# Attention over the unmasked tokens: projections a head earlier, one token transpose per head, gathers two batches ahead, all token sums on GpSimd

## What is computed

```python
xt = jnp.transpose(x, (0, 2, 1))
q = xt @ Wq.T                                   # 8 heads of 64
scores = scale * jnp.einsum('bhqd,bhkd->bhqk', qh, qh)
logits = (scores * cmask + (1.0 - cmask) * NEG) * rmask
attn = jax.nn.softmax(logits, axis=-1)
ctx = jnp.einsum('bhqk,bhkd->bhqd', attn, qh)
out = ctx @ Wo.T
x = x + jnp.transpose(out, (0, 2, 1))
```

## Time and profile before

| | us |
|---|---|
| median of 3 runs (1754.6 to 1766.28) | 1764.37 |
| the profiled execution | 1761.67 |
| its span, first to last instruction | 1759.9 |
| prologue and front, up to the first batch's loop | about 98 |
| one batch, mean of fifteen | 102.7 |

### The profile page before, as it was taken

The page is one execution under the profiler, slowest core; times in us unless marked ns, Lnnn a source line. Parts: engine busy times, 40 slices in busy tenths (PEclk is TensorE's granted clock), DMA queues, the critical chain, the costliest instruction groups (busy, mean ns, idle before and its releaser), DMA issues. The chain is left out here.

```text
span 1759.9 us, 33141 instructions
## 1 busy us (share of the span) xinstructions
PE 1585.6 (90%) x10956; PEld 1243.4 (71%) x10956; DVE 1285.5 (73%) x2794; ACT 853.9 (49%) x2055; POOL 1244.2 (71%) x979
## 2 busy tenths in 40 slices
PE   6798998989899898989989898998989899898995
PEld 3667777777777676767767677777777677677763
DVE  5458686777768687786877768687786868778673
ACT  1145554544555445455544545555454555545451
POOL 5266785868678587767868677686877768687672
PEclk9689999999999999999999999999999999999997
DMA  3244443535434354443444434344443534444320
GB/s 121 63 102 97 97 121 78 137 85 122 109 78 125 85 129 102 105 125 68 126 94 123 102 90 122 92 120 99 111 113 90 133 81 121 99 112 114 72 77 27
DMA packets 93809, 179.08 MB, mean 102 GB/s; under 512 B 24705, under 2 KB 24833, under 8 KB 93633
## 3 DMA queue, kind: packets, MB, share of 16 engines
q1 hardware_dynamic: 64448, 109.71, 27.1%
q0 software_dynamic: 29184, 67.17, 13.7%
HBM read 36.77 MB, written 33.55 MB: 40 GB/s over the span
## 5 line engine op out<-in xcount | busy, mean ns | idle before, releaser
L752 ACT ACTIVATE small_Pt<-scores,small_kbias 108x270 f32<-108x270 f32 x1280 | 552.6, 484 | 650.8 <-PE scores L1098 589.1
L884 DVE TENSOR_REDUCE small_mxp<-max_scores 108x1 f32<-108x270 f32 x1280 | 548.4, 433 | 313.9 <-PE max_scores L1080 295.0
L598 POOL TENSOR_TENSOR small_Pacc<-small_Pacc,small_Pt 108x540 f32<-108x540 f32 x384 | 521.1, 1357 | 223.7 <-ACT small_Pt L752 210.2
L1080 PE MATMUL max_scores<-small_ops 128*108 128x270 f32 x1280 | 435.3, 343 | 85.8 <-DMA small_ops<-small_L 43.1
L1080 PEld LDWEIGHTS max_scores<-small_ops 128*108 128x108 f32 x1280 | 226.4, 177 | 206.2 <-issue 77.3
L1110 PE MATMUL ctx_psum<-small_Pt,small_V 108*64 108x270 f32 x2560 | 313.0, 391 | 0.0
L914 DVE RECIPROCAL small_rsum<-small_rsum 128x67 f32<-128x67 f32 (+1 forms) x512 | 240.5, 532 | 57.3 <-ACT small_rsum L696 57.3
L1095 PE MATMUL scores<-small_ops 128*108 128x270 f32 x1280 | 275.0, 295 | 4.6 <-ACT small_Pt L752 3.1
L1098 PE MATMUL scores<-small_ops 128*108 128x270 f32 x1280 | 267.8, 291 | 0.0
L598 POOL TENSOR_TENSOR small_Pacc<-small_Pt 108x540 f32<-108x540 f32 x128 | 171.8, 1342 | 133.4 <-ACT small_Pt L752 128.6
L1110 PEld LDWEIGHTS ctx_psum<-small_Pt,small_V 108*64 108x64 f32 x2560 | 184.0, 137 | 107.5 <-issue 0.6
(11 more groups left out here) (106 smaller groups left out, 2316.9 us busy)
## 6 DMA issues: line engine op xcount, KB each, us to landing
small_ops<-small_H SPq DMA_DIRECT2D x512, 135.0 KB
small_ops<-small_L SPq DMA_DIRECT2D x256, 135.0 KB
small_ops<-small_mrow SPq DMA_DIRECT2D x128, 2.1 KB
small_xg<-x_rows,small_idx POOLq DMA_INDIRECT x80
small_xtail<-x_rows,small_idx POOLq DMA_INDIRECT x80
out_rows<-small_xtail,small_idx POOLq DMA_INDIRECT x80, 3.1
out_rows<-small_xg,small_idx POOLq DMA_INDIRECT x80
wq_sb<-wq SPq DMA_DIRECT2D x1, 1024.0 KB, 5.6
```

What stands on the lines that cost most here:

```text
L598: nc.gpsimd.tensor_tensor(acc, other, t["Pt"][:R, p0], ALU.add).then_inc(pacc_step, 1)
L752: nc.scalar.activation(t["Pt"][:R, (NT * s + k) % f.NP, half, :], ST[(2 * (NT * h + k) + half) % 3][:R, 0:H], ACT.Exp, bias=t["kbias"][:R, ...
L884: nc.vector.tensor_reduce(t["mxp"][:R, h % 2, m // 2, m % 2:m % 2 + 1], MX[m % 2][:R, 0:H], AX.X, ALU.max).then_inc(mx_red, 1)
L1080: nc.tensor.matmul(MX[m % 2][:R, 0:H], ops[:, OPA, tile_cols(m // 2)], ops[:, OPB, half_cols(m % 2)], start=True, stop=True).then_inc(mx_r ...
```

## The change

Six edits.

1. `PAIR_STEPS`: pair 3's first half from (0,4) to (0,3)-(0,4); pair 4's halves from (4,4) and (5,0)-(5,1) to (4,3) and (4,4); pair 5's first from (5,4) to (5,3)-(5,4).
2. `V_STEPS`: each of the two V parts has a place of its own. `XT_STEPS`: the token transposes go from (4,0) to (4,2), all in one head, to one in each of heads 1, 2 and 3, always (h,2) part 1, and two in head 4. The mean goes from (7,1) to (6,2), part 1.
3. Main tiles are gathered two batches ahead, in heads 6 and 7 (the third token buffer was there already), tail tiles one batch ahead in heads 2 and 3; a semaphore for even and one for odd batches. The prologue gathers batch 1 too. `MASKED_AT` goes from (3,3), (3,4) to (0,0), (0,1).
4. All token sums after the first batch's are on GpSimd: tail tiles in heads 4 and 5, the main tiles of the batch after next in head 7.
5. The masks of all 16 batches are made by three operations in the prologue.
6. The output tile is finished in place and not by way of the sum buffer, and the transposes use one identity matrix for both types.

```diff
 PAIR_STEPS = [
-    ((0, 0), (0, 1), "proj", (2, 1)), ((0, 4), (0, 4), "proj", (3, 0)), ((1, 0), (1, 1), "proj", (3, 1)),
+    ((0, 0), (0, 1), "proj", (2, 1)), ((0, 3), (0, 4), "proj", (3, 0)), ((1, 0), (1, 1), "proj", (3, 1)),
...
-    ((4, 4), (4, 4), "proj", (4, 0)), ((5, 0), (5, 1), "proj", (4, 1)), ((5, 4), (5, 4), "proj", (5, 0)),
+    ((4, 3), (4, 3), "proj", (4, 0)), ((4, 4), (4, 4), "proj", (4, 1)), ((5, 3), (5, 4), "proj", (5, 0)),
...
-V_STEPS = {1: (0, 3), 2: (4, 3), 3: (5, 3), 4: (6, 3)}
-XT_STEPS = [(4, 0, 0), (4, 0, 1), (4, 1, 0), (4, 1, 1), (4, 2, 0)]
-XBAR_STEP = (7, 1, 1)
+V_STEPS = {1: ((0, 2, 1), (0, 3, 0)), 2: ((4, 0, 0), (4, 0, 1)), 3: ((5, 0, 0), (5, 1, 0)), 4: ((6, 3, 0), (6, 4, 0))}
+XT_STEPS = [(1, 2, 1), (2, 2, 1), (3, 2, 1), (4, 1, 0), (4, 2, 1)]
+XBAR_STEP = (6, 2, 1)
...
-MASKS_AT = (2, 4, 1)
-MASKED_AT = [(3, 3), (3, 4)]
+MASKED_AT = [(0, 0), (0, 1)]
...
-VECTOR_SUM_AT = {1: (5, 0, 1), 2: (5, 1, 0), 3: (5, 1, 1), 4: (5, 4, 1), 5: (6, 0, 1), 6: (6, 1, 0)}
-POOL_SUM_AT = {7: (6, 1), 8: (6, 3), 9: (6, 4)}
+ADD_W_AT = [(0, 0), (0, 1), (0, 3), (0, 4), (1, 0)]
+SCATTER_TAIL_AT = [(1, 1), (1, 3), (1, 4), (2, 0), (2, 1)]
+GATHER_TAIL_AT = [(2, 3), (2, 4), (3, 0), (3, 1), (3, 3)]
+SCATTER_AT = [(3, 4), (4, 0), (4, 1), (5, 0), (5, 1)]
+TAIL_SUM_AT = [(4, 3), (4, 4), (5, 2), (5, 3), (5, 4)]
+GATHER_AT = [(6, 0), (6, 1), (6, 3), (6, 4), (7, 0)]
+SUM_AT = [(7, 1), (7, 2), (7, 3), (7, 4)]
+FIRST_SUM_AT = [(2, 1), (2, 2), (3, 1), (3, 2)]
...
                 def finish_tile(b, par, k, bank):
...
-                    nc.vector.scalar_tensor_tensor(out=t["xsum"][:R], in0=MB[bank][:R, 0:D],
-                                                   scalar=t["valid"][:R, slot, k:k + 1], in1=xk, op0=ALU.mult,
+                    nc.vector.scalar_tensor_tensor(out=xk, in0=MB[bank][:R, 0:D],
+                                                   scalar=t["valid"][:R, b, k:k + 1], in1=xk, op0=ALU.mult,
...
+                nc.vector.tensor_tensor(t["valid"][:], j, n, ALU.is_lt).then_inc(masks_made, 1)
+                nc.vector.tensor_tensor(t["inv"][:], j, n, ALU.is_ge).then_inc(masks_made, 1)
+                dve.wait_ge(masks_made, 2)
+                nc.vector.tensor_scalar(t["kbias"][:], t["inv"][:], NEG, None, ALU.mult).then_inc(masks_made, 1)
```

More of the change, by code:

```diff
@@ L111, in misc_jobs @@
     if form.split:
[L112 removed]
+        for pair, places in V_STEPS.items():
             if pair < PAIRS or has_next:
[L114 to L115 removed]
+                for i, (h, k, part) in enumerate(places):
+                    whole(part, "V", (pair, i), (h, k))
         for first, last, name, arg in PAIR_STEPS:
@@ L166, in pool_jobs @@
             if has_next:
-                table[GATHER_TAIL_AT[i]].append(("gather", NT + i))
+                table[GATHER_TAIL_AT[i]].append(("gather", 1, NT + i))
+                table[TAIL_SUM_AT[i]].append(("sum_tokens", 1, NT + i))
         for i in range(NT):
@@ L170, in pool_jobs @@
                 table[SCATTER_AT[i]].append(("scatter", i))
[L171 to L176, removed]
+            if has_third:
+                table[GATHER_AT[i]].append(("gather", 2, i))
+        for i in range(1, NT):
+            if has_third:
+                table[SUM_AT[i - 1]].append(("sum_tokens", 2, i))
+            if not has_prev:
+                table[FIRST_SUM_AT[i - 1]].append(("sum_tokens", 1, i))
         return table
@@ L184, in pool_jobs @@
         for i in range(NT):
-            table[gathers[i]].append(("gather", i))
+            table[gathers[i]].append(("gather", 1, i))
         for i in range(1, NT):
-            table[4 + (i - 1) // 3, (i - 1) % 3].append(("sum_tokens", i))
+            table[4 + (i - 1) // 3, (i - 1) % 3].append(("sum_tokens", 1, i))
     return table
@@ L567, in job @@
                     elif name == "gather":
-                        gather(b + 1, arg)
+                        gather(b + ahead, arg)
                     elif name == "add_w":
@@ L617, in body @@
                 nc.gpsimd.memset(t["ops"][DK:DK + 1, :, OPY, :].bitcast(F32), 1.0).then_inc(ops_cleared, 1)
+                if f.split:
+                    for k in range(NT):
+                        gather(1, k)
                 def batch(b, par, table, has_prev, has_next):
-                    jobs = pool_jobs(f, has_prev, has_next)
+                    jobs = pool_jobs(f, has_prev, has_next, b + 2 < B)
                     for h in range(HEADS):
@@ L624, in batch @@
                                 add_tile(HEADS * b + h, h, k)
-                            for name, arg in jobs[h, k]:
-                                job(name, arg, b, par)
+                            for name, *ahead, arg in jobs[h, k]:
+                                job(name, ahead[0] if ahead else 0, arg, b, par)
                 def tail(jobs):
@@ L1199, in job @@
                         row = CT[:NT, H:H + R] if f.split else mb[:NT, 0:R]
-                        nc.tensor.transpose(row, t["mcol"][:R, arg % 2, :], ident[:R, :R]).then_inc(mT_ready, 1)
+                        nc.tensor.transpose(row, t["mcol"][:R, arg % 2, :], identR[:R, :R].bitcast(F32)).then_inc(mT_ready, 1)
                     elif name == "L":
```

81 lines of the change are left out of this document (28 added, 53 removed).

## The result

| | before | changed |
|---|---|---|
| median, us | 1762.69 (1754.6 to 1766.28, 4 runs) | 2050.36 (2049.24 to 2050.8, 4 runs) |
| ratio, 95% interval | | 1.1635 (1.161 to 1.1661) |
| span of the profiled execution, us | 1759.9 | 2048.2 |

A forecast was written before the change was run, and what follows sets the result against it. TensorE's waits were taken to decide: 17.0 + 1.7 - 6.0 = 12.7 us a batch, 191 in 15 batches, plus 3 for the last and 46 for the clock, 240 in all, giving 2004 us; range 1870 to 2075.

The forecast's parts named there:

- The path: At (h,2), ScalarE copies row sums after value products, transposes and their copies, delaying VectorE; long waits total 17.0 us a batch.
- that of the banks: Experiments' rival theory: transposes and output products alternating on two banks cause the wait, whatever the sums' order; no chance given.
- Rival C: In heads 1 to 3 TensorE waits only for the reduction behind the reciprocals, one step later: 1885 us; chance 0.12.
- Rival A: The long path doesn't bind, or TensorE's waits overlap, so only the removals count: 1657 us; chance 0.06.
- Rival B: GpSimd sets the pace, its head 7 sums delaying L (the row-sum matmul): 1717 us; chance 0.03.
- D: Rival: long waits are a quarter of those worked out and cancel against the removals: 1764 us; chance 0.03.
- The waits for the low part: TensorE waits for VectorE's token tile low half: 3.7 us in heads 1 to 3, 3.1 at head 4's projection.
- the row maxima: In heads 0 and 6, maxima wait for the reduction behind the reciprocals: 1.4 us each, 2.8 a batch.
- L's 1.7 us: Row-sum matmul L waits for its bank: 0.6 us each in heads 2 and 3, 0.5 in heads 0, 1 and 6.
- The clock: New long waits lower TensorE's granted clock: 0 to 92 us, the upper being four times as much low clock; 46 taken.
- The removals: Operand wait, mean's wait, transposes' bank queue and half VectorE's wait go: 6.0 us a batch, 7.0 with clock.
- the projection's place: Pair 4's second projection ends at (4,4) instead of (5,1), removing the row maxima's operand wait: 2.9 us a batch.

The follow-up runs named there:

- e1: Changed kernel with ScalarE serving the row sums ahead of the step's other copies at (h,2): 1703.06 us, 0.9672 of before.
- e2: Changed kernel with head 0's V part, the transposes and the mean at (h,2) moved from part 1 to part 0: 1665.16 us, 0.9454 of before.
- e5: Kernel of e2 with head 0's V part and the mean back in part 1, ScalarE serving row sums ahead of their copies: 1637.41 us.
- e7: Kernel of e2 with six of a batch's nine token sums back on VectorE, four in head 7, two in head 4: 1699.14 us.
- e3: Changed kernel with the score products of (h,3) repeated six times in heads 1 to 3, five in head 4, to fill TensorE's waits: 1949.2 us.
- e6: Kernel of e2 with pair 4's projection halves back at (4,4) and (5,0) to (5,1), as before the change: 1676.52 us.
- e9: Kernel of e6 with three token sums on VectorE in head 5, at (5,0), (5,1) and (5,1): 1706.03 us.
- e4: Changed kernel with ScalarE's 0.63 us refill of the token tile buffer behind the row sums in heads 1 to 3: 2045.58 us.
- e10: Kernel of e2 with three token sums on VectorE in head 5, at (5,0), (5,1) and (5,1): 1721.1 us.

## Why the prediction was right, point by point

**Direction and mechanism: right, and shown.** The path goes as worked out. Counted from the start of the transposes (651.91 in the working, 736.19 in the changed trace):

| | worked out | measured |
|---|---|---|
| cast starts | 0.55 | 0.62 |
| row sums end | 2.06 | 2.14 |
| next reduction starts | 3.9 | 3.97 |
| low half ends | 4.8 | 4.85 |
| output product's wait | 3.7 | 3.70 |

The prediction's theory and that of the banks are kept apart by e1 and e2, which cure the two ends of the same order and both bring the time under before's. Rival C, that the output product's bank would not be what TensorE waits for, falls by the row that names it. Rival A named the right price for the removals alone: 1657, where e2 has 1665 and e5 1637, but its condition doesn't hold. Rival B falls by the changed kernel's waits, where L waits 0.3 us for GpSimd in all, and by e7; D falls by the result.

**Idle time: right within a tenth.** I had 12.7 us more a batch; 19.8 - 8.2 = 11.6 were measured. The waits for the low part were to be 3 x 3.7 + 3.1 = 14.2 a batch, 213 in all. The row has 204.5: fourteen batches have them as worked out, but the first batch has no output products, and so only the projection's wait, which I overlooked. At the row maxima I took 1.4 us each; head 6 has 1.47, head 0 has 1.07. L's 1.7 us is (15.9 + 11.3 + 7.6)/15 = 2.3 against 0.25 before; 7.6 of it is head 4's, where L takes the bank of a token tile, which I left out.

**The clock: this is the term that was mis-sized.** I bounded it at 0 and 92 us and took 46. Of 289 us, 15 x 11.6 = 174 are idle time, where the sum had 194, which leaves 115 for the clock, above even the upper bound of 92; e3 takes 101 away. The step that failed is "four times as much" as the upper bound, made from one long wait a batch. Low clock rose from 127 to 389 us in all, and in the stretches from 4.1 a batch to (1 - 0.91) x 2 x 1722/14 = 22, more than five times. In the 3.4 us behind the wait the clock was under 1.00 for every one of the long waits, and in all fifteen batches also for the 1.47 us wait of head 6, which I had not counted among its causes. For the 1.07 us wait of head 0 it stayed at 1.00 in all fifteen. Here is head 6 of batch 2, and below it the stretch behind head 0's wait in batch 3:

```profile
436.31 0.38 PE L1065 MATMUL max_scores<-small_ops 128*108 128x270 f32 x1 [1.47 <-DVE small_mxp L866]
436.60:440.00 3.40, 3.25 (x16) 2.97 (x15) 2.48 (x7) 1.98 (x6) 2.23 (x3) 0.51 0.47 118
...
462.32:465.72 3.40, 3.20 (x24) 3.02 (x25) 3.07 (x9) 2.40 (x6) 2.73 (x3) 1.00 0.35 79
```

So the range held the result by its upper part: forecast 2004, measured 2050. The clock was 69 us over its term and the idle time 20 under its own, and it was luck that the two errors partly cancel. By the Trainium skill, TensorE: Matmul & The Clock Gate, section on HAM oscillation, work parted by waits starts slow after each of them. That rule was nearer than my middle. The trace agrees for the 57 waits of 3.2 and 3.7 us and for the 1.47 us wait of head 6, not for the 1.07 us wait of head 0; e3 agrees too: waits filled, 121 us of low clock.

**The removals: right in sum, not in their parts.** 7 us a batch, clock included, were forecast for a kernel without the long path; e2 shows 97.5/15 = 6.5, e5 8.3. But I gave 2.9 us of it to the projection's place and 1.1 to VectorE's freed time. The runs say 11.4 us in all, 0.8 a batch, for the first (e6) and 34 us, 2.3 a batch, for the second at e7's places. The other 3.4 of the 6.5 no run takes apart: the mean, the spread transposes, the gathers and the masks together. In the earlier trace rows I read a wait for a DMA and took the projection's place as its cause, without following the copies back to the low part and that to the sums ahead of it on VectorE. That the sums in head 5 delay that low part is shown by e9 (1.8 us at L); that this was what made 2.0 of the old 2.9 us is inferred from e6 and e9, for no run put the old wait back at the operands.

## What to carry to other kernels

When hand-written lists drive several engines, compare for each step the order in which the producer makes results with the order in which each consumer serves them; a consumer that serves an early result behind a late one turns the whole distance into a wait, and here one sort key was worth 347 us. Moving work to a place where it looks hidden is safe only if what is queued behind its consumers can wait too. Price a new wait of a few microseconds on TensorE at more than its length (here 289 us for 174 of idle time), don't count on getting the clock's part back in proportion, and follow a wait for a DMA back to what allowed the copy to be issued.

## What was not expected of the hardware

**The same time with less waiting.** e4 has 25.5 us less waiting than the changed kernel and 31 us more low clock. From the fourth batch on both settle at 122 to 124 us a batch, most of them at 122.9, though e4 waits 1.8 us less in each: (3 x 3.7) - (3 x 3.1). The traces show where it goes. Read in steps of 0.25 us from 450 to 1064 us, five batches, both have 25 stretches at the low level. In the changed kernel four of them are twice as long as the others, in e4 ten are, together 99 us against 119.5. What makes one stretch longer than another isn't settled.

**VectorE's adds beside GpSimd's.** In the same trace of before, the token add of 108x512 took VectorE 683 ns on average for the tail tiles and 1512 for the main tiles:

```profile
L879 DVE TENSOR_TENSOR small_xsum<-small_xsum,small_xg 108x512 f32<-108x512 f32 x48 | 72.6, 1512 | 0.7 <-issue 0.3
L879 DVE TENSOR_TENSOR small_xsum<-small_xsum,small_xtail 108x512 f32<-108x512 f32 x34 | 23.2, 683 | 0.3
```

In e10 the tail tiles' adds, moved to head 5, have a mean of 1527:

```profile
L867 DVE TENSOR_TENSOR small_xsum<-small_xsum,small_xtail 108x512 f32<-108x512 f32 x49 | 74.8, 1527 | 0.4
```

What GpSimd does meanwhile tells them apart. In the trace of before, 30 of these adds ran while GpSimd did nothing and 15 beside a gather alone: all took 0.68 to 0.69 us. The 28 that began while GpSimd was accumulating probability tiles took 1.03 to 1.72, and some that an accumulation joined later up to 2.55. In e10 the 14 with nothing beside them took 0.68 us, the 27 beside an accumulation and a gather or scatter 1.47 to 2.54. Meeting an accumulation isn't enough by itself: in e9, 14 adds that began just ahead of one took 0.68. That the accumulation causes the longer add was not isolated by a run. The longer adds go with the 56 us by which e10 is slower than e2: 45 adds of 1.5 us make 69 us, ahead of reductions that TensorE waits for; the lower clock (0.962 against 0.979) is in the 56 too. On GpSimd the same add took 1282 ns, with nobody waiting: moving it there took it off VectorE at less than its price beside an accumulation.
